# A local-attention and MLP stack on one Trainium2 core: TensorE's program put into loops of two steps, and a token shift moved from ScalarE to DMA

## What is computed

```python
x = x + 0.5 * ffn(layernorm(x))          # six layers
x = x + linear_recurrence(layernorm(x))  # in, scan over tokens, out
x = x + 0.5 * ffn(layernorm(x))          # the same six layers
...
# one layer of ffn
x = attn_layer(shift_tokens(x), Wqkv, q_scale, k_scale, Wo) + x
x = ffn_layer(shift_tokens(x), g, b, W1, b1, W2, b2) + x
```

## Time and profile before

| | us |
|---|---|
| median of 3 runs (3302.3 to 3308.17) | 3307.57 |
| the profiled execution | 3317.88 |
| its span, first to last instruction | 3316.0 |
| PE / DVE / ACT / POOL busy | 3177.3 / 2748.5 / 2545.5 / 2226.4 |
| PEld busy | 2384.7 |
| mean granted TensorE clock, share of full | 0.995 |

### The profile page before, as it was taken

The page is one execution under the profiler, slowest core; times in us unless marked ns, Lnnn a source line. Parts: engine busy times, 40 slices in busy tenths (PEclk is TensorE's granted clock), DMA queues, the critical chain, the costliest instruction groups (busy, mean ns, idle before and its releaser), DMA issues. The chain is left out here.

```text
span 3316.0 us, 150147 instructions
## 1 busy us (share of the span) xinstructions
PE 3177.3 (96%) x63272; PEld 2384.7 (72%) x63464; DVE 2748.5 (83%) x6951; ACT 2545.5 (77%) x4144; POOL 2226.4 (67%) x1453
## 2 busy tenths in 40 slices
PE   7999999999999999999999999999999999999997
PEld 4777777777777777777777777777777777777776
DVE  7888888888888888889998888888888888888885
ACT  3777777777777777777777777777777777777775
POOL 6666666666666666667887666666666666666663
PEclk9999999999999999999999999999999999999999
DMA  4111111111111111111111111111111111111111
GB/s 124 45 48 45 48 44 48 45 48 45 47 42 43 48 45 48 45 48 45 47 39 45 48 44 48 45 46 41 45 48 45 48 44 48 45 44 43 47 52 38
DMA packets 135089, 157.39 MB, mean 47 GB/s; under 512 B 75539, under 2 KB 108439, under 8 KB 134423
## 3 DMA queue, kind: packets, MB, share of 16 engines
q1 hardware_dynamic: 129815, 144.42, 15.7%
q10 hardware_dynamic: 4608, 3.34, 0.3%
HBM read 33.38 MB, written 1.05 MB: 10 GB/s over the span
## 5 line engine op out<-in xcount | busy, mean ns | idle before, releaser
L1073 POOL TENSOR_TENSOR rot<-rot,swp 128x1024 f32<-128x1024 f32 x384 | 907.0, 2362 | 137.8 <-DVE rot L866 137.8
L482 PE MATMUL proj<-wq,xsT 128*128 128x512 f32 x1536 | 769.6, 622 | 27.6 <-DVE rot L866 10.3
L673 ACT ACTIVATE sq<-proj 128x512 f32<-128x512 f32 x768 | 438.0, 596 | 416.1 <-PE proj L482 406.3
L1082 POOL TENSOR_TENSOR rot<-rot,rn 128x1024 f32<-128x1024 f32 x384 | 724.4, 1908 | 0.0
L1063 POOL TENSOR_TENSOR rt<-rt,half 128x1 f32<-128x1 f32 x192 | 105.3, 549 | 755.6 <-DVE rt L936 755.6
L860 DVE TENSOR_TENSOR swp<-proj,tab 128x512 f32<-128x512 f32 x768 | 521.3, 679 | 12.2 <-ACT sq L673 7.2
L866 DVE TENSOR_TENSOR rot<-proj,tab 128x512 f32<-128x512 f32 x768 | 517.9, 674 | 0.8 <-PE tps L493 0.8
L990 DVE SCALAR_TENSOR_TENSOR hT<-proj,cols,fg 114x128 f32<-114x128 f32 (+1 forms) x576 | 166.7, 345 | 417.7 <-ACT fg L739 413.6
L493 PEld LDWEIGHTS tps<-idf,rot 128*128 128x128 f32 x3072 | 360.2, 141 | 206.2 <-issue 204.1
L1067 POOL TENSOR_TENSOR prob<-prob,rr 128x1024 f32<-128x1024 f32 x192 | 365.4, 1903 | 174.9 <-DVE rr L948 174.9
L482 PEld LDWEIGHTS proj<-wq,xsT 128*128 128x128 f32 x1536 | 259.8, 190 | 254.9 <-issue 145.4
(11 more groups left out here) (102 smaller groups left out, 5873.0 us busy)
## 6 DMA issues: line engine op xcount, KB each, us to landing
vb<-va SPq DMA_DIRECT2D x192, 384.0 KB, 3.5
vb<-va SPq DMA_DIRECT2D x192, 128.0 KB, 3.6
wq<-in_L_ffn_Wqkv SPq DMA_DIRECT2D x95, 192.0 KB, 3.4
xs<-Z SPq DMA_DIRECT2D x192, 32.0 KB
wo<-in_L_ffn_Wo SPq DMA_DIRECT2D x94, 64.0 KB, 2.8
xs<-Z SPq DMA_DIRECT2D x192, 28.0 KB
xs<-Z SPq DMA_DIRECT2D x192, 3.8 KB
xs<-Z SPq DMA_DIRECT2D x192, 0.2 KB
```

The costliest lines, as they stand in the source:

```text
L482: mm(proj[:, c % 2, :], xsT[:, k.parity(L_QKV), 0:P], wq2[:, bass.ds(w + c * 512, 512)], start=True, stop=True).then_inc(p_qkv[c], 1)
L673: fn(sq[:, c * 512:(c + 1) * 512], proj[:, c % 2, :], ACT.Square).then_inc(a_sq[c], 1)
L1073: g_.tensor_tensor(r, r, swp[:, g * INNER:(g + 1) * INNER], ALU.add).then_inc(g_add[g], 1)
L1082: g_.tensor_tensor(r, r, rn[:, g * HEADS:(g + 1) * HEADS].unsqueeze(2) .to_broadcast([P, HEADS, DH]), ALU.mult).then_inc(g_nm[g], 1)
```

## The change

PE's program is no longer written out for most steps. `pipeline_by_layer` makes a `Fori` loop of two steps per pass for each layer (steps 7 to 84 and 113 to 190, ten loops, 78 passes), and the start, the steps with the recurrence and the end stay written out. The step is rotated: what was its first part, the projections 1 and 0 (`head`), now stands at the end of a pass, for the step that follows, and a pass begins with the rest (`body`). Within a layer's loop the MLP's first weights have a fixed address.

The token shift of the attention input is made by four DMAs from `Z` into a new buffer `xs`, two tiles long, one step ahead (`L_DX` = -1). PE transposes `xs`, and ACT's three instructions become one copy. The other engines' programs stay written out.

```diff
+L_DX = -1
...
-        xsT = sb("xsT", [2, 1 + P])
+        xs = sb("xs", [2, P])
+        xsT = sb("xsT", [2, P])
...
+        d_xs = [sem(f"d_xs{g}") for g in range(2)]
...
-        def pipeline_by_layer(eng, step, between=None):
+        def pipeline_by_layer(eng, head, body, between=None):
+
+            def unrolled_body(first, end, between=None):
+                for s in range(first, end):
+                    body(Step(eng, None, s, {}))
+                    if between is not None:
+                        between(s)
+                    head(Step(eng, None, s + 1, {}))
 
             at = L_F + UNROLL
-            unrolled(eng, step, 0, at, between)
+            head(Step(eng, None, 0, {}))
+            unrolled_body(0, at, between)
             for layer in range(LAYERS):
                 end = min(L_F + (layer + 1) * TILES, T)
                 if layer == DEPTH - 1:
-                    unrolled(eng, step, at, MID_END + 1)
-                    at = MID_END + 1
+                    unrolled_body(at, MID_END + 4)
+                    at = MID_END + 4
                 else:
                     many = (end - at) // UNROLL * UNROLL
-                    looped(eng, step, at, at + many, layer % DEPTH)
+                    odd = at % 2
+                    with eng.Fori(at - odd, at + many - odd, UNROLL) as i:
+                        memo = {}
+                        for j in range(UNROLL):
+                            body(Step(eng, i, odd + j, memo, layer % DEPTH))
+                            head(Step(eng, i, odd + j + 1, memo, layer % DEPTH))
                     at += many
-            unrolled(eng, step, at, T + L_F2)
+            unrolled_body(at, T + L_F2)
...
+                next_tile(k)
                 load_weights(k)
...
+            def next_tile(k):
+
+                if k.on(L_DX):
+
+
+                    k.wait(v_z, L_DX)
+                    k.wait_mid(m_z, TILES + L_DX)
+                    k.wait(p_xT, L_X + 1)
+                    shift(k, L_DX, xs[:, k.parity(L_DX), :], d_xs[k.parity(L_DX)])
+
             sp.wait_ge(c_zero2, 1)
+            next_tile(Step(sp, None, L_DX, {}))
...
-                    k.wait(v_z, L_X)
-                    k.wait_mid(m_z, TILES)
-                    tr(tps[:, 4, :], Z[:, bass.ds(k.slot(L_X), P)], idf[:, :]).then_inc(p_xT, 1)
+                    k.wait_pair(d_xs, L_X, 64)
+                    tr(tps[:, 4, :], xs[:, k.parity(L_X), :], idf[:, :]).then_inc(p_xT, 1)
...
-            pipeline(pe, step)
+            pipeline_by_layer(pe, head, body)
...
-                    hf, par = P // 2, k.parity(L_X)
-                    cp(xsT[0:hf, par, 0:P], tps[0:hf, 4, :])
-                    cp(xsT[hf:P, par, 1:P + 1], tps[hf:P, 4, :])
-                    k.wait(a_xT, L_X + 1)
-                    fn(xsT[hf:P, par, 0:1], xsT[hf:P, 1 - par, P:P + 1], ACT.Copy,
-                       scale=0.0 if k.tile(L_X) % POS == 0 else 1.0).then_inc(a_xT, 1)
+                    cp(xsT[:, k.parity(L_X), :], tps[:, 4, :]).then_inc(a_xT, 1)
...
-                    k.wait(p_xT, L_WO)
+                    k.wait_pair(d_xs, L_WO - 1, 64)
```

More of the change, by code:

```diff
@@ L481, in project @@
                 w = k.layer_parity(L_QKV, 3 * INNER)
-                mm(proj[:, c % 2, :], xsT[:, k.parity(L_QKV), 0:P],
+                mm(proj[:, c % 2, :], xsT[:, k.parity(L_QKV), :],
                    wq2[:, bass.ds(w + c * 512, 512)], start=True, stop=True).then_inc(p_qkv[c], 1)
@@ L487, in values @@
                 w = k.layer_parity(L_S, 3 * INNER)
-                mm(proj[:, c, :], xsT[:, k.parity(L_S), 0:P], wq2[:, bass.ds(w + (4 + c) * 512, 512)],
+                mm(proj[:, c, :], xsT[:, k.parity(L_S), :], wq2[:, bass.ds(w + (4 + c) * 512, 512)],
                    start=True, stop=True).then_inc(p_v[c], 1)
@@ L542, in attend, with head @@
                 last.then_inc(p_O, 1)
-            def step(k):
+            def head(k):
                 if k.on(L_QKV):
@@ L556, in step, with body @@
                         project(k, c)
-                if k.s == 3:
+                if k.reg is None and k.s == 3:
                     idle(4)
+            def body(k):
                 if k.on(L_AV):
@@ L565, in step @@
                     k.wait_mid(m_x2, M_OUT + 1)
-                if k.s in (1, 2):
+                if k.reg is None and k.s in (1, 2):
                     idle(2)
@@ L1013, in _ @@
             v.memset(kT[:, :, 2 * P:2 * P + WIN], 0.0)
-            v.memset(xsT[:, 1, P:P + 1], 0.0)
             v.memset(va[:, 1, :], 0.0).then_inc(c_zero, 1)
```

## The result

| us | before | after |
|---|---|---|
| median | 3306.74 (4 runs) | 3267.94 (3267.78 to 3271.3, 4 runs) |
| profiled execution | 3317.88 | 3267.87 |
| its span | 3316.0 | 3266.1 |

The ratio of the medians is 0.9887, 95% interval 0.987 to 0.9904: 38.8 us less, 1.2%, where I had forecast 64.6 less. The sign was right, and 3268 lies in the range. That range was widened to reach into rival B and is a weak test; 3268 also lies in the forecast's own range of 3206 to 3286.

What follows compares the result with a forecast made beforehand. PE, busy in 96% of the span, was taken as the bound, with 79.0 us of instruction-fetch stalls. 3317.9 - 68.9 - 11.5 + 15.6 = 3253.1, from the median 3243 us; range 3215 to 3480 us.

Steps and rivals of the forecast that it cites:

- rival B: At each loop's end, every jump back waits for an instruction fetch and sequential fetches continue: 3507 us, slower; chance 0.33.
- (a): PE's 156 looped steps: loops remove instruction-fetch stalls, 68.9 us saved of 79.0.
- first end: In PE's loops, a pass's blocks stay in instruction memory, nothing fetched after the first pass: 68.9 us saved.
- (b): In PE's looped steps, the jump and register instructions only the sequencer executes cost 0.10 us a step, 15.6 us lost.
- The sequencer works ahead of PE and most of it is hidden: In PE's loops, about 50 added instructions, 5 us per pass of 33, are mostly covered by queued PE work.
- the one with no room: Second value projection L488: only 0.06 us to spare after its wait for VectorE, with a register instruction added there.
- Rival C: At three late places of a step, register instructions eat the gain: 3297 us, within 3285 to 3330; chance 0.10.
- (c): Token shift before the projections: one shorter ScalarE copy saves 0.06 us in each of 192 steps, 11.5 us.
- so I carry differences over: Profiled execution of 3317.9 us lay 10.3 above the median, so the predicted difference was subtracted from the median 3307.6.
- D: At the loops' jumps, targets are fetched yet hidden and no stall goes: 3312 us, no change; chance 0.03.

Runs made afterwards that it cites:

- run 2: Changed kernel's loops, but the token shift made by ScalarE's three instructions as before, after one straight transfer from Z to xs; 3269.92 us, ratio 0.9878.
- run 3: Changed kernel with the seam not rotated: a pass ends behind the scores and the projections start the next; 3296.86 us, ratio 0.996.
- run 5: Changed kernel with the registers for the next step's projections 1 and 0 computed behind the output projection instead of behind the scores; 3254.78 us, ratio 0.9832.
- run 6: run 5's kernel with addresses of projections and value projections computed before their waits, which the matmuls carry; also called version 6; 3252.32 us, ratio 0.9818.
- run 7: Changed kernel with four more, long-satisfied waits per looped step, behind the scores and ahead of projections 1 and 0; 3305.01 us, ratio 0.9981.
- run 8: Changed kernel with the same four added waits as run 7, but behind the output projection; 3280.87 us, ratio 0.9912.
- run 9: Changed kernel again, unaltered, in one session with run 10; 3271.46 us, ratio 0.9888.
- run 10: run 6's kernel again, unaltered, in one session with the changed kernel; 3250.17 us, ratio 0.9826.
- run 4: Changed kernel with passes of four steps in place of two, 38 passes of 10.6 blocks of 256 instructions; 3509.85 us, ratio 1.06.
- run 1: Token shift by transfers and single copy alone, PE's program written out in its old order as in the kernel before; 3302.7 us, ratio 0.9979.
- run 11: run 4's passes of four steps, with a hint at the top of each pass announcing the jump at its end; 3421.57 us, ratio 1.034.

## Why the prediction was right, and where it was off

**(a) The loops, first end: right.** Packets fell to 156 (forecast: some 170, with six for each of ten loops; by the eleven there are, some 174), 60 of them in the looped stretches, where 413 were. Runs 2, 3 and 5 to 10, all with passes of 5.3 blocks, have 156, and run 4 with 10.6 has 570. So a pass of 5.3 blocks stays in TensorE's instruction memory and one of 10.6 is fetched anew each time. The Trainium skill's page Runtime: NRT & Kernel Launch, section Instruction fetch mechanics, has both numbers that I weighed: its 128 KiB would be eight blocks, and every run agrees, though none lies between 5.3 and 10.6; its rule that a taken branch out of the current two pages forces a fetch does not hold in this kernel, whose 67 taken jumps go back over five blocks (no `COMPARE_BRANCH` above 258 ns).
What the two stretches hold above the steps without a stall was 2637.4 - 78 x (16.424 + 16.363) = 80.0 us before and is 2584.7 - 78 x (16.552 + 16.526) = 4.6 after. So 75.4 us are gone by the profile, where I had 68.9; most first passes met no stall. Of the 80 us the view of waits shows 63.9 as PE's idle time; how the rest arises no run shows.

**(b) The register instructions: mis-sized, and the main step that failed.** "The sequencer works ahead of PE and most of it is hidden" was drawn from one place, a block's entry 1.4 us before PE ran dry. Behind the scores it fails. I had called the second value projection "the one with no room". It costs what I had given it: from run 5 to run 6 the step falls by 0.09 us, at that place, against the 0.10 booked. The term that I had at nothing is the seam behind the scores, where the sequencer has just issued 256 instructions in 1.5 us and is 0.1 us ahead: once it is relieved, in run 5, the step falls by another 0.09. A looped step takes 16.54 us against 16.36 written out, and 0.18 x 156 is 28 us, not 15.6. Run 5, which moved only the seam's instructions, has looped stretches 13 us shorter than the change; runs 6 and 10, with the waits moved too, 18 and 21, and their step is as short as a written-out one. The missing 7 to 10 us come back as stalls, most of them in first passes (steps 21, 53, 70, 149 and 181 are 0.7 to 2.0 us longer than the others in both). Run 7 shows the same from the other side. Rival C was thus right in kind, and less than half its size.

**(c) The token shift: half the size alone, nothing in company.** Run 1 has 0.035 us a step, as only every second step gains; I had read the length and the slack off one step, which is of the longer kind. In the loops the shift is worth nothing (run 2), because what (b) adds stands at the same seam, and of two things that end close together only the later counts: without the shift the loops lose 0.15 us a step (16.54 against 16.39), with it 0.18 (16.54 against 16.36). I had added the two terms as if they stood at different places. Whether the shift is worth its 0.035 us again in version 6, where the seam is relieved, no run shows. SP's queue behaved as described: the four for `xs`, two for weights, four for `xs2`, with room between.

```profile
1006.15 0.42 SPq L375 DMA_DIRECT2D wo<-in_L_ffn_Wo  x1
1008.38 0.52 SPq L419 DMA_DIRECT2D xs<-Z  x1
```

It is idle from 1006.57 to 1008.38, 1.8 us (forecast 1.9), and VectorE's list of waits has no DMA of size.

**The sum, by the profiled executions.** Forecast 3253.1, measured 3267.9, so 14.8 too little: -6.5 from (a) (75.4 for 68.9), +12.7 from (b) (28.3 for 15.6), +6.0 from (c) (156 x 0.035 = 5.5 for 11.5), +2.8 from the rest of the program; rounding leaves 0.2.

**The base.** The other 10 us of the miss come from "so I carry differences over". The profiled execution before lay 10.3 us above its median, the profiled one after lies at its own. If the surplus was stalls, it went with them and should not have been subtracted from the median a second time; that it was is argued and not shown, though run 1's profile has 10.6 us less of the scores' stalls in code of the same length. That step turned 15 us of error in the mechanism into 25 in the time.

**Rival B** was wrong for this loop and right for one of twice the length. I had it at 0.33, and what decides is whether the pass fits. Its price of 1.5 us exposed was too small even there: the jump takes 3.8 us, not 2.6, PE idles 3.2 us before the transposes (96.2 in 30 times), and the clock is at 1.2 GHz behind it. **D** did not occur.

## What to carry to other kernels

Here a loop that removes instruction fetches paid where its body fitted the engine's instruction memory, and cost more than it could save where it did not; count the instructions of a pass before anything else, and look at the instruction packets and the longest compare-and-branch afterwards. Put the jump behind long matmuls, compute addresses before the wait and not between wait and matmul, nor right behind many small matmuls. Count the sequencer's instructions in the trace and not the waits in the code. Two savings at one seam don't add, and a term made of stalls belongs to the execution in which they were counted.

## What the hardware showed that I had not expected

- TensorE's sequencer has almost no lead behind dense small matmuls: 0.1 us at the end of 256 instructions in 1.5 us. Instructions that only it executes take 0.09 to 0.16 us each from start to start there, a satisfied wait of 0.051 us included (0.11, run 7); ahead of a late wait they cost nothing (run 8, the step with the jump).
- A taken compare-and-branch to a target in memory took 213 ns in the median, 0.27 us to the sequencer's next instruction; an untaken one 81 ns and 0.14. The Trainium skill's page Advanced Engine Details and Errata, section Control Flow Timing, has about 108 ns, which is half of what this trace shows for a taken one.
- A jump to a block that is not in memory took 3.8 us (run 4), more than the 2.6 of a sequential fetch, and after idle stretches of about 3 us TensorE's granted clock stood at 1.2 GHz for 3.4 to 10.2 us.
- The announced jump took 2.1 us in the median of the 27 taken, instead of 3.8, with a spread from 0.6 to 3.8 (run 11): the hint, given ten blocks ahead, helps some passes and not others. Which, and why, stays open.
